# Graph layers on one Trainium2 core: the prologue of the next graph laid between the late pieces of the current one, a bank of its own for the dense layer, and the fine index spread by DMA

## The reference, cut to what matters

```python
rank = jnp.cumsum(ni, axis=-1) - ni
nb = ni.sum(-1)
rem = neigh & (sk > 1) & (rank % sk == sk - 1) & mask[:, :, None]
rem = rem | jnp.swapaxes(rem, 1, 2)
adj_d = jnp.where(rem, 0.0, adj_)
s = jnp.sort(jnp.where((adj_d > 0)[..., None], x[:, None, :, :], jnp.inf), axis=2)
for tau, w in zip(TAUS, WTS):                  # 0.25, 0.5, 0.75
    pos = tau * jnp.maximum(nv - 1, 0)         # nv: neighbours that are left
    agg = agg + w * (v_lo + frac * (v_hi - v_lo))   # the two order statistics around pos
y = relu((x + agg) @ W1 + b1) @ W2 + b2
x = layernorm(x + y * mask)
```

## Time and profile before

| | |
|---|---|
| median of 3 runs | 4057.33 us (4055.46 to 4057.52) |
| profiled execution, its time | 4058.42 us |
| profiled execution, its span | 4056.5 us |
| VectorE busy | 3547.8 us, 87% |
| TensorE matmuls busy | 2739.0 us, 68% |
| ScalarE busy | 2124.7 us, 52% |
| all DMA queues | 55.45 MB, 14 GB/s |
| chain that ended last | VectorE 56%, TensorE 28%, ScalarE 8% |

### The profile page before, as it was taken

One profiled execution on the slowest core, in us unless ns is written; L12 is line 12 of the kernel. 1 busy time (PEld: TensorE's weight loads), 2 busy tenths in 40 slices (PEclk: granted clock), 3 DMA queues, 4 the chain that ended last, 5 costly groups with the idle time before them and its releaser, 6 DMA issues.

```text
span 4056.5 us, 45358 instructions
## 1 busy us (share of the span) xinstructions
PE 2739.0 (68%) x15690; PEld 1141.2 (28%) x15690; DVE 3547.8 (87%) x6052; ACT 2124.7 (52%) x3063; POOL 63.1 (2%) x50
## 2 busy tenths in 40 slices
PE   0000043978777777878796969696969696877897
PEld 0000021322323232323232323232323232323665
DVE  7999989989898989898989898989999898954676
ACT  1112343756566666657474747474747474654132
POOL 0005000000000000000000000000000000000000
PEclk6555566989798989898888979797979797978777
DMA  1010000000000000000000000000000000000011
GB/s 23 0 41 0 0 6 18 1 23 11 13 11 13 11 13 11 13 11 13 13 11 13 11 24 1 23 1 23 1 23 10 14 11 13 1 8 6 32 39 34
DMA packets 138096, 55.45 MB, mean 14 GB/s; under 512 B 120328, under 2 KB 123546, under 8 KB 137882
## 3 DMA queue, kind: packets, MB, share of 16 engines
q1 hardware_dynamic: 133754, 51.67, 5.0%
q10 hardware_dynamic: 4128, 1.05, 0.2%
HBM read 39.07 MB, written 13.63 MB: 13 GB/s over the span
## 4 chain that ended last, share of the span: by engine, by line
DVE 56%; PE 28%; ACT 8%; issue 7%; DMA 0%; DVEq 0%; ACTq 0%
PE rows L548 6%; DVE picked L1188 6%; PE ring L520 6%; DVE prod L1137 5%; PE found_bank L557 3%; ACT hot L847 3%; DVE picked L1177 2%; PE bcast L535 2%; DVE keys L1011 2%; DVE keys L1010 2%; DVE late L1165 2%; DVE member L1077 2%; PE bcast L536 2%; DVE perm L1033 2%; ACT below L825 2%
## 5 line engine op out<-in xcount | busy, mean ns | idle before, releaser
L847 ACT ACTIVATE hot<-bcast,eq_bias 128x1024 bf16<-128x1024 f32 x768 | 859.0, 1118 | 29.9 <-PE bcast L536 29.5
L548 PE MATMUL rows<-hot,table 128*64 128x512 bf16 x4608 | 681.9, 403 | 158.5 <-DVE prod L1137 158.5
L1137 DVE SCALAR_TENSOR_TENSOR prod<-near,iota_b,rows 128x512 f32<-128x512 bf16 x768 | 572.0, 745 | 129.6 <-PE rows L548 115.1
L843 ACT ACTIVATE near<-bcast 128x512 bf16<-128x512 f32 x768 | 458.6, 597 | 245.0 <-DVE prod L1137 124.0
L557 PE MATMUL found_bank<-prod,sum_to 128*64 128x512 f32 x1536 | 467.5, 650 | 94.5 <-DVE prod L1137 94.5
L520 PE MATMUL ring<-member,neigh_t 128*128 128x512 bf16 x2048 | 509.8, 386 | 17.3 <-ACT words L817 17.3
L532 PE MATMUL bcast<-idx_bt,sel_b 128*128 128x512 bf16 x768 | 309.5, 403 | 188.3 <-ACT near L843 177.3
L1188 DVE TENSOR_TENSOR picked<-picked 128x6144 uint16<-128x6144 uint16 (+2 forms) x192 | 387.8, 2020 | 0.7
L548 PEld LDWEIGHTS rows<-hot,table 128*64 128x64 bf16 x4608 | 216.6, 111 | 586.1 <-issue 500.0
L535 PE MATMUL bcast<-idx_t,sel_a 128*128 128x512 f16 x768 | 309.2, 403 | 102.5 <-ACT hot L847 101.8
L449 PE MATMUL ring<-ident,swapped 128*128 128x128 f32 x32 | 6.4, 366 | 507.2 <-DVEq L994 507.2
(11 more groups left out here) (324 smaller groups left out, 4279.4 us busy)
## 6 DMA issues: line engine op xcount, KB each, us to landing
late<-in_adj_dram SPq DMA_DIRECT2D x16, 1024.0 KB, 5.4
adjt_d<-late SPq DMA_DIRECT2D x16, 512.0 KB, 2.9
adj_l<-adjt_d SPq DMA_DIRECT2D x16, 512.0 KB, 4.2
adj_s<-adjt_d SPq DMA_DIRECT2D x16, 512.0 KB, 3.6
parts_d<-parts SPq DMA_DIRECT2D x6, 512.0 KB, 5.1
table<-parts_d SPq DMA_DIRECT2D x192, 16.0 KB, 2.2
out_dram<-x_all SPq DMA_DIRECT2D x4, 512.0 KB, 3.8
x_all<-in_x_dram ACTq DMA_DIRECT2D x2, 512.0 KB, 8.8
```

The source lines that it names most:

```text
L548: ins = mm(rows[u % 2][C * h:C * h + C, :], table[:, s, 2 * g8 + h, :], hot[:, u % HOT, h, :], start=(s == 0), stop=(s == 2))
L843: run(near[:, u % DEEP], bcast[:, 2, :], ACT.Copy).then_inc(S["near_ready"], 1)
L847: run(hot[:, u % HOT].rearrange(flat), bcast[:, 0:2, :].rearrange(flat), ACT.Relu, bias=eq_bias[:, :]).then_inc(S["hot_ready"], 1)
L1137: stt(out=prod[:, u % DEEP, :], in0=near[:, u % DEEP, :], scalar=iota_b[:, :], in1=rows[u % 2][:, :], op0=ALU.is_equal, op1=ALU.mult).then ...
```

## The change

- **Prologue.** The body of a graph is cut into `select(b)` and `region(t, p, l, d)`. In `region`, the bits of graph `t = b`, the prologue of graph `p = b + 1`, the dense layers of graph `d` and the last 15 units of lookup `l` alternate piece by piece on every engine. The first chunks of tile 0 of graph `p` are made at its end.
- **Places of the units.** `PLACES` puts 4 units in tile 0 (after its four wide operations), 9 in tile 1, 10 in tiles 2 and 3 (33 before `region`, the constant `LATE`). After the index has been turned, `select` on TensorE makes four chunks of tile 1 before the first spread, and on ScalarE the three masks of tile 1 stand ahead of the first `hot`.
- **Banks.** The dense layers write `dense_bank`, the third part of `bcast`, which the spread of the fine index has left. The adjacency matrix is turned through `ring` and not through `bcast`.
- **Fine index.** The matmul L532 and the eviction L843 are gone, and with them the matrix `sel_b`. For each unit SyncE issues a DMA that reads 8 partitions of `idx_bt` sixteen times and writes the 128 partitions of `near` (128 KB), which now has six buffers. These DMAs stand in SyncE's one order with the loads and stores of the adjacency matrices and the table.
- **Selection of VectorE** is in a new order (`pick(2)`, the starts, `pick(1)`, `pick(0)`), because `idx` moves to the front of `picked`; `pick(1)` waits for the turned index. `weight` has two halves.

```diff
-BEFORE, PER_STEP = 10, 7
+NEAR = 6
+PLACES = ((6, 7, 8, 9), (1, 2, 3, 4, 5, 6, 7, 8, 9), tuple(range(10)), tuple(range(10)))
+LEAD = [sum(len(p) for p in PLACES[:i]) for i in range(NT + 1)]
+LATE = LEAD[NT]
+        dense_bank = bcast[:, 2, :]
@@ SyncE
+            def places(l, lo, hi):
+                for u in range(lo, hi):
+                    k, g8 = divmod(u, GROUPS)
+                    row = (k % 2) * C + 8 * g8
+                    if u == 0:
+                        hold(sp, S["idxT_ev"], TURNS * l + TURNS, S["sp_passed"])
+                    if u >= NEAR:
+                        hold(sp, S["prod_ready"], UNITS * l + u - NEAR + 1, S["sp_passed"])
+                    sp.dma_start(near[:, u % NEAR, :],
+                                 idx_bt[row:row + 8, k // 2, :].unsqueeze(1).to_broadcast([8, 16, N])).then_inc(near_in[u % NEAR], 16)
...
@@ TensorE
             def spread(l, u):
-                mm(bcast[:, 2, :], sel_b[:, 16 * row:16 * row + P], idx_bt[:, k // 2, :], start=True, stop=True).then_inc(S["place_ps"], 1)
...
+            def select(b, l):
+                for n in range(4):
+                    chunk(b, 1, n)
+                if l is not None:
+                    spread(l, 0)
+                    spread(l, 1)
+                for n in range(4, CW):
+                    units(l, LEAD[0] + n - 3)
+                    chunk(b, 1, n)
+                for i in range(1, NT):
+                    for s in range(10):
+                        if i + 1 < NT and s < CW:
+                            chunk(b, i + 1, s)
+                        units(l, LEAD[i] + s + len(PLACES[i]) - 9)
...
+            def region(t, p, l, d):
...
+                units(l, LATE + 13)
+                if p is not None:
+                    pe.wait_ge(S["member_ready"], NT * p + NT)
                     for n in range(CW):
                         if n == 1:
+                            pe.wait_ge(S["nv_read"], p + 1)
+                        chunk(p, 0, n)
+                        if n == 3:
+                            units(l, LATE + 14)
                 units(l, UNITS)
...
@@ ScalarE
             def spread(l, u):
-                act.wait_ge(S["place_ps"], UNITS * l + u + 1)
-                if u >= DEEP:
-                    act.wait_ge(S["prod_ready"], UNITS * l + u - DEEP + 1)
-                run(near[:, u % DEEP], bcast[:, 2, :], ACT.Copy).then_inc(S["near_ready"], 1)
...
+            def select(b, l):
                 if l is not None:
                     run(x_now[:, :, :], xb(l), ACT.Copy).then_inc(S["x_copied"], 1)
+                chunk(b, 1, 0)
+                chunk(b, 1, 1)
+                for k in range(TAUS):
+                    mask(b, 1, k)
+                chunk(b, 1, 2)
+                chunk(b, 1, 3)
                 units(l, 2)
...
@@ VectorE
             def value(l, u):
+                dve.wait_ge(near_in[u % NEAR], 16 * (UNITS // NEAR * l + u // NEAR + 1))
                 dve.wait_ge(S["row_ps"], UNITS * l + u + 1)
...
+            def region(t_of, p, l, d):
+                units(l, LATE)
+                if t_of is not None:
+                    bits_start()
+                units(l, LATE + 1)
+                if p is not None:
+                    members(p, 0)
+                units(l, LATE + 2)
+                if t_of is not None:
+                    bits_first(l)
+                if d is not None:
+                    ffn_end(d)
+                units(l, LATE + 4)
+                if p is not None:
+                    clear_own(p)
...
+                units(l, LATE + 12)
+                if t_of is not None:
+                    bits_last()
+                if d is not None:
+                    gcn_end(d)
+                if p is not None:
+                    limits(p)
+                units(l, LATE + 13)
+                if t_of is not None:
+                    bits_next(t_of, l)
+                    tell("idx_ready")
```

More of the change, by code:

```diff
@@ L281, in build @@
         S = {n: sem(n) for n in names}
+        near_in = [sem(f"near_in{q}") for q in range(NEAR)]
         adjs_in = [sem(f"adjs_in{q}") for q in range(SLOTS)]
@@ new lines, in select @@
+                chunk(b, 1, 0)
[4 more added lines that the diff above has]
+                chunk(b, 1, 3)
+                units(l, 2)
+                for n in range(4, CW):
+                    units(l, LEAD[0] + n - 3 + 2)
+                    chunk(b, 1, n)
+                for i in range(1, NT):
+                    for s in range(10):
+                        if i + 1 < NT and s < CW:
+                            chunk(b, i + 1, s)
+                            if s in (3, 4, 5):
+                                mask(b, i + 1, s - 3)
+                        units(l, LEAD[i] + s + len(PLACES[i]) - 9 + 2)
@@ L892, in body, with region @@
+            def region(t, p, l, d):
+                if l is not None and t is None:
+                    run(x_now[:, :, :], xb(l), ACT.Copy).then_inc(S["x_copied"], 1)
+                units(l, LATE + 2)
                 if d is not None:
                     hidden(d)
-                units(l, at + 2)
+                units(l, LATE + 5)
+                if p is not None:
+                    convert(p)
+                    keep_turned(p)
                 if d is not None:
                     root_of(d, 0)
-                units(l, at + 4)
+                units(l, LATE + 7)
@@ L1146, in select, with place, pick @@
             def select(b, i, l):
-                at, cnt = BEFORE + PER_STEP * i, cnt2[:, i % 2]
+                cnt = cnt2[:, i % 2]
+                last, starts = (G - 1) * C, picked[:, 3].bitcast(BF16)
+                def place(p):
+                    units(l, LEAD[i] + sum(1 for n in PLACES[i] if n <= p))
+                def pick(w):
+                    did(tt(picked[:, w], below[:, i % 2], change[:, w, :].unsqueeze(1).to_broadcast([P, TAUS, G * C]), ALU.mult))
                 dve.wait_ge(S["cw_ev"], NT * CW * b + CW * i + 2)
-                last, starts = (G - 1) * C, picked[:, 3].bitcast(BF16)
                 need(count[0])
@@ L1189, in select @@
                     n //= 2
-                    units(l, at + (6 if n == G * C // 4 else 7))
+                    place({256: 7, 128: 8, 64: 9}[n])
                 did(tt(result[:, :, i, :, :], picked[:, :, :, 0:C], picked[:, :, :, C:2 * C], ALU.bitwise_xor))
```

448 lines of the change are left out of this document (219 added, 229 removed).

## The result

The changed kernel takes 4097.53 us (median of 4, 4093.62 to 4101.1), the kernel before beside it 4056.95 us: a ratio of 1.010, 95% interval 1.0083 to 1.0118. It is slower by 40 us, on the side and by the way that the prediction gave, and 28.5 us above its 4069. The net forecast was +12 us, a small difference of two sums near 200, so that errors of a few per cent in them move it by its own size.

A forecast was written before the change was run, and what follows sets the result against it. VectorE was taken to bound the kernel nearly everywhere, so only its waits could change: 4058.4 - 189 + 214 - 13 = 4070, and with the median 1.1 us below the profiled execution 4069 us; range 3980 to 4135.

The forecast's parts named there:

- The net forecast: Whole kernel: 189 us of VectorE waits go, 214 us of new waits come, and the last lookup gives -13 us.
- What goes: Prologue: VectorE's waits on other engines go once its pieces alternate with others in `region`, 12.6 us per graph, 189 us.
- The six rows: VectorE's waits in one graph: tile 0's last and first chunks, `apart_of`, lookups, kept edges; 12.8 us, nearly all in the prologue.
- The start of the selection: First lookups of a graph: `prod` waits 6.5 us behind chunks, masks and first `hot`, then 0.5; 15 times, 105 us.
- The end of `region`: Lookup 46 behind four chunks of tile 0 waits 3.0 us, lookup 39 0.3 us; 14 times, 46 us.
- The tiles: Tiles 1 and 2: four closely spaced `prod` wait, 2.1 us lost in each, tile 3 nothing; 15 times, 63 us.
- The last lookup: Last graph's lookup: without L532 a unit takes 1.85 us and not 2.13, over 46 units -13 us.
- Rival C: Near transfers from 8 partitions set the pace in last lookup and tiles, 2.9 us each: 4149 us; chance 0.12.
- B: Turned index and four chunks: TensorE keeps full clock and in-order slack is larger, so faster, 4005 us; chance 0.34.
- D: Tile 1: TensorE stays at half speed, three lookups after the first lose 4 us, +52, 4120 us; chance 0.11.

## Why the prediction was right, and by how much it was short

**What goes: right.** The six rows are gone, and the lookups that wait now are counted below. They were 12.8 us in the graph shown, some 190 us in fifteen.

**The start of the selection: right in its mechanism, short by 0.7 us.** 7.0 us was budgeted, 6.5 at the first `prod` and 0.5 behind it; measured 7.7 and nothing. The steps hold: the index is evicted 6.5 us after TensorE is released, the second chunk at 10.8 (forecast for half speed), the first `hot` at 17.2 (the late end of its forecast), and VectorE arrives at 14.4 (14.2 forecast). From the end of that `hot` to the end of the first lookup it took 4.8 us where I had 4.4 at half speed, so the wait came out above even my high end of 7.4. And I had taken a value between the ends for full and for half clock, although the rows show the lookup's matmuls at 0.84 or at 1.50 us: the pause was there, and the half-speed end was the likely one.

**The end of `region`: the same.** 3.3 us forecast, 3.6 + 0.5 = 4.1 measured at lookups 46 and 39. My high end for lookup 46 was 3.9.

**The tiles: right, a little high.** 2.1 us forecast and 1.9 measured in each, in three waits and not in four. That ScalarE's order makes most of them is shown.

Together 14.5 us were forecast per graph and 15.6 came in the graph shown. These 1.1 us are what lies between the net of 1.7 us forecast (25 us in fifteen graphs) and the 2.7 measured: **the mis-sized terms are the two at half clock**, 0.7 and 0.8 us, less 0.4 for the tiles; 16 us in all. The 2.7 is an average in which the first period, with -4.0 us where the same terms give -1.4, hides that the others cost 3.2.

**A term that was left out: the last graph's `region`.** It is 9.1 us longer, and my sum had nothing for it. By its start 33 lookups are done and not 38, so it has five more `prod`, 3.3 us. The rest is in the trace as waits, 7.5 us for 1.6 before, most of it in three:

```profile
3579.74 0.75 DVE L1192 SCALAR_TENSOR_TENSOR prod<-near,iota_b,rows 128x512 f32<-128x512 bf16 x1 [1.88 <-PE rows L563]
...
3603.93 0.75 DVE L1192 SCALAR_TENSOR_TENSOR prod<-near,iota_b,rows 128x512 f32<-128x512 bf16 x1 [2.45 <-PE rows L563]
...
3612.76 0.75 DVE L1192 SCALAR_TENSOR_TENSOR prod<-near,iota_b,rows 128x512 f32<-128x512 bf16 x1 [2.09 <-PE rows L563]
```

No run takes these away. What comes ahead of the fourth tile of graph 0, without lookups, gave 4.0 us back, which I had not counted either.

**The last lookup: less than forecast.** -13 us forecast, about -8 measured: 1.99 us per unit (pairs of 1.81 and 2.17), where 1.85 was forecast and 2.13 was before. TensorE is busy 53.5 us of 60 and no longer the bound; the ring of spread and `hot` is, and `hot` waits 0.70 and 1.06 us in turn, since in every second unit the sums stand in front of the spread.

**Rival C fell.** No `prod` waits for `near` in the changed kernel: the last lookup moved one transfer every 1.99 us, where C took 2.9 us, and 131 KB / 1.99 us is 66 GB/s. By the Trainium skill ("SBUF — State Buffer", "Door 1: The DMA port swizzle") eight neighbouring partitions would give 54.4 GB/s and one transfer 2.4 us, an estimate from that page; the trace does not agree, and the measurement goes beyond the rule. The 2.5 us that the forecast took from issue to landing was too short, by the run with two buffers, which alone shows it, as the trace names no landing for these transfers; six buffers hid it.

**Rivals B and D.** B failed at its premise, the full clock: the chunks ran at half speed. Even where added matmuls brought them to full clock, the first wait was 6.0 us. D (half speed into tile 1) did not come: the lookups after the first take 0.84 us.

Open: why TensorE answers at lookup 39 at half speed in some graphs and kernels and not in others. In the changed kernel the wait there goes from nothing to 2.26 us from graph to graph, with one order; the mean is 0.6 us there, and 1.3 to 1.9 in five of the kernels with an edit. That the wait is made by the lookup's place behind the count is shown, and in two graphs the clock beside it; what sets the clock there is not.

## What to carry to other kernels

Work moved out of one pause of the bounding engine must be weighed with the queues of the engines that serve it: here waits of 12.8 us per graph went and 15.7 us came, by the order in which ScalarE and TensorE served the rest; other orders of the same work took 203 us off. Order each serving engine's queue by when the bounding engine wants the result, and look at the next three requests, not at the first. Where a forecast hangs on the clock of an engine that comes from a pause, take the half-speed end, not a mean. And read a wait over all graphs before sizing an edit: the one at lookup 39 ran from nothing to 2.3 us.

## What was not expected of the hardware

Matmuls added to keep TensorE at full clock did so (3.71 us for 6.38), but it was at half speed again after the next idle stretch, of 4.85 us; they brought 9 us, and 40 only together with a lookup moved elsewhere, of which some 9 are the move's own. With two buffers a transfer of 128 KB, from 8 partitions spread over 128, has landed 4.7 us after its release, yet one every 1.99 us is sustained. And 100 MB more of transfers cost VectorE nothing that the trace shows: its busy time per graph is 176.6 us before and 176.3 after.
